# Self-attention probabilities transposed by VectorE blocks and SBUF transfers instead of TensorE, with a reordered step

## The chip, the cores and the metric

One core of a Trainium2 chip runs the whole kernel. The metric is device time in microseconds, median of several runs. Five engines run their own programs and meet only at semaphores: TensorE (PE, matrix products into PSUM), VectorE (DVE), ScalarE (ACT), GpSimd (POOL), and SP, which here issues nearly all DMA transfers, in the order of its program.

## The reference

64 sequences of 64 tokens with 512 features pass through one block of a transformer, everything in float32:

```python
x = x + xattn(layernorm(x), ctx, ctx, mask)   # 16 heads of 32, 512 context keys each
x = x + attn(layernorm(x))                    # self-attention over 64 tokens, 16 heads
x = x + ffn(layernorm(x))                     # relu(x W1 + b1) W2 + b2, W1 and W2 rounded to -1, 0, 1
```

The change lies in the second line. For each head q, k and v are projections with a bias, the scores are q k / sqrt(32), their softmax runs over 64 keys (the top-k mask keeps all 64), the probabilities multiply v, and the result goes through an output projection with a bias and is added to x.

## The kernel before

It has three stages, cross attention (to about 736 us), self attention (to about 1205 us) and FF, and every engine walks through them with a program of its own, written by hand, with explicit waits (`wait(e, semaphore, count)`). Nothing is scheduled by a planner: the order in `self_pe`, `self_act`, `self_dve`, `self_pool` and `self_sync` is the order in which the engines work.

The self stage goes through 16 units of four sequences, each in two tiles t = 0, 1 of 128 tokens (L447, `load_self_x`). Steps 0 and 1 stand out, a hardware loop runs steps 2 to 13, then come a last but one and a last step (`run_steps`). Step u is pipelined over three units: it attends in unit u, projects q, k and v of unit u+1, and makes the layer norm of unit u+2. Each projection is split into high and low parts, 12 or 24 products (`split_products`, L348), and goes to one of the banks `PJ`, whose turn is counted by `Banks`. Names of the products: Q0, Q1, K0, K1 (halves of the features), V0, V1, O0, O1 (tiles; O is the output projection). O1 of a unit is done in the next unit's step.

For one tile: `scores` on PE (L544), `self_maxima` on DVE (row maximum L519, subtraction L521), `self_exponentials` on ACT (L527), `self_divide` on DVE (sum L532, reciprocal, product L420), eight `transposes` of 128 x 128 on PE (L1460) into the PSUM pair PT, `probs_t_out` on ACT (L1596), which copies them to SBUF, `attend` on PE (L1481), `a_hi` and `a_lo`, which split the result into two parts (L1584 on ACT, L1657 and L1661 on DVE), and the O product. DVE adds O to the residual (`residual`, L1680), SP stores it (L1425).

The layer norm of unit u+2 takes, in step u: the load of x by SP (L447), statistics (L453) and aggregate on DVE, rstd on POOL (`rstd_of`, L1246), normalise (L465) and block transpose (L428) on DVE, a gather of four transfers on SP (L436), `x_hi` on ACT and `x_lo` on DVE (L556). POOL's step has two parts in this order, `self_residuals` for unit u+1, which adds x and the output bias into the buffer that unit u-1 has used and so waits for both stores of u-1, and then `rstd_of` for unit u+2:

```python
if kind != "last":
    self_residuals(e, later(u, 1))
if kind == "full":
    rstd_of(e, G.agg, G.eps, G.rstd, later(u, 2), NT, P)
```

In step u DVE works in the order: maxima (tile 0), residual O1 of u-1, statistics of u+2, divide (0), aggregate, maxima (1), normalise, a_hi and a_lo (0), divide (1), layer-norm transpose, K1 copy, V0 copy, two ternary columns of FF weights (L1301, L1304), V1 copy, x_lo, residual O0, a_lo (1). SP: load x of u+2, store (u-1, 1), layer-norm gather of u+2, store (u, 0). The cross stage already transposes its probabilities by DVE blocks of 32 x 32 (L1105) and four SBUF to SBUF transfers (L634).

## Time and profile before

| | us |
|---|---|
| median of 3 runs | 1671.46 (1671.02 to 1673.8) |
| profiled execution, its own time | 1671.81 |
| its span, first to last instruction | 1670.0 |
| mean granted TensorE clock | 0.988 of full |
| PE busy | 1604.1 (96%) |
| DVE busy | 1139.2 (68%) |
| ACT busy | 635.6 (38%) |
| POOL busy | 229.3 (14%) |

The span is that of one execution under the profiler. PE's busy share is an average over the three stages; what a change in one stage does is read in that stage, from which wait ends last there. A wait is put down to the engine or transfer whose signal came last.

### The profile page before, as it was taken

What the parts mean: (1) busy time and instruction counts of PE and PEld (TensorE: products, weight loads), DVE (VectorE), ACT (ScalarE), POOL (GpSimd) and SP (SyncE); (2) the same over time, 40 slices, a digit from 0 to 9 for tenths busy, and PEclk for the clock granted to TensorE, in tenths of its full rate; (3) what the DMA queues carried; (4) which work ended last, traced back from release to release, by engine and by line L of the source; (5) the groups of instructions that cost most, each with busy time, mean ns of one, the idle gap of its engine ahead of it and who ended that gap; (6) DMA issues with size and microseconds to landing.
All of it is one profiled execution on the core that took longest, in us unless ns stands there. A gap on an engine that the chain in (4) does not pass through costs nothing.

```text
span 1670.0 us, 37711 instructions
## 1 busy us (share of the span) xinstructions
PE 1604.1 (96%) x15500; PEld 1340.4 (80%) x15500; DVE 1139.2 (68%) x1556; ACT 635.6 (38%) x1593; POOL 229.3 (14%) x300
## 2 busy tenths in 40 slices
PE   5899999999999999969999999999799999999999
PEld 4678888888888887758888889888688888888887
DVE  3677777777777777856787777877686446555633
ACT  2555555555555555545222223222222222122221
POOL 1000000001111111311211112121122102202200
PEclk9999999999999999989999999999899999999999
DMA  6144444444444445463112121122212112211100
GB/s 228 39 113 116 115 113 113 113 115 118 116 116 113 113 114 139 145 236 96 46 51 63 38 69 44 50 63 77 58 51 69 58 26 76 63 57 31 51 26 26
DMA packets 120304, 144.61 MB, mean 87 GB/s; under 512 B 11936, under 2 KB 85792, under 8 KB 118944
## 3 DMA queue, kind: packets, MB, share of 16 engines
q1 hardware_dynamic: 120080, 139.32, 29.2%
q10 hardware_dynamic: 144, 4.19, 0.7%
q8 instruction: 53, 0.87, 0.2%
q14 instruction: 27, 0.22, 0.0%
HBM read 67.97 MB, written 25.17 MB: 56 GB/s over the span
## 4 chain that ended last, share of the span: by engine, by line
PE 87%; DVE 7%; DMA 2%; ACT 1%; issue 1%; SPq 1%; POOL 0%; DVEq 0%; ACTq 0%
PE project L348 49%; PE project L1351 14%; PE scores L1831 3%; PE scores L1829 3%; PE project L1831 3%; PE project L1829 3%; PE scores L775 3%; PE attended_t L794 2%; PE project L1460 2%; PE attended_t L1481 1%; DMA cross_probs_t<-cross_scores_probs 1%; PE scores L544 1%; SPq L634 1%; DVE cross_row_max L1088 1%; DVE self_at_lo L1661 1%
## 5 line engine op out<-in xcount | busy, mean ns | idle before, releaser
L1351 PE MATMUL project<-ff_xt,w_ternary 128*128 128x512 f32 x1024 | 253.1, 389 | 0.0
L1351 PEld LDWEIGHTS project<-ff_xt,w_ternary 128*128 128x128 f32 x1024 | 192.0, 188 | 39.8
L1361 ACT ACTIVATE hidden<-project,b_sb 128x512 f32<-128x512 f32 x128 | 88.2, 689 | 339.3 <-PE project L1351 339.3
L959 ACT ACTIVATE cross_scores_probs<-cross_scores_probs,exp_bias,logit_scale 128x128 f32<-128x128 f32 x256 | 123.0, 482 | 139.1 <-DVE exp_bias L1093 139.1
L348 PE MATMUL project<-self_xt_hi,self_w_hi 128*128 128x256 f32 x512 | 149.2, 291 | 2.4 <-DVE self_w_lo L408 2.4
L348 PE MATMUL project<-self_xt_lo,self_w_hi 128*128 128x256 f32 x512 | 146.2, 285 | 0.0
L348 PE MATMUL project<-self_xt_hi,self_w_lo 128*128 128x256 f32 x512 | 146.0, 285 | 0.0
L959 ACT ACTIVATE cross_probs<-cross_scores,exp_bias,logit_scale 128x128 f32<-128x128 f32 x256 | 122.8, 484 | 4.5 <-DVE exp_bias L1093 4.5
L348 PE MATMUL project<-ctx_hi,cross_w_hi 128*128 128x512 f32 x256 | 105.6, 412 | 15.8 <-DVE ctx_lo L1118 15.8
L348 PE MATMUL project<-cross_w_hi,ctx_hi 128*128 128x512 f32 x256 | 105.5, 412 | 0.0
L348 PEld LDWEIGHTS project<-self_xt_hi,self_w_hi 128*128 128x128 f32 x512 | 99.4, 194 | 4.9 <-issue 2.9
L348 PE MATMUL project<-ctx_hi,cross_w_lo 128*128 128x512 f32 x256 | 101.8, 398 | 0.0
L348 PE MATMUL project<-ctx_lo,cross_w_hi 128*128 128x512 f32 x256 | 101.5, 396 | 0.0
L1366 DVE CAST hidden_hi_a<-hidden 128x512 fp32r<-128x512 f32 x64 | 28.9, 452 | 105.4 <-ACT hidden L1361 105.3
L348 PE MATMUL project<-cross_w_lo,ctx_hi 128*128 128x512 f32 x256 | 100.5, 392 | 0.0
L481 POOL TENSOR_TENSOR self_residual<-self_x,bo_sb 128x512 f32<-128x512 f32 x32 | 53.9, 1708 | 335.6 <-DMA x<-self_residual 335.6
L348 PEld LDWEIGHTS project<-self_xt_lo,self_w_hi 128*128 128x128 f32 x512 | 99.4, 194 | 0.6
L348 PE MATMUL project<-cross_w_hi,ctx_lo 128*128 128x512 f32 x256 | 99.6, 389 | 0.0
L348 PEld LDWEIGHTS project<-self_xt_hi,self_w_lo 128*128 128x128 f32 x512 | 99.5, 194 | 0.0
L1366 DVE CAST hidden_hi_b<-hidden 128x512 fp32r<-128x512 f32 x64 | 28.7, 449 | 88.4 <-ACT hidden L1361 87.5
L1255 POOL TENSOR_TENSOR var_eps<-mean_var,ln_eps 128x2 f32<-128x2 f32 x16 | 5.1, 318 | 572.6 <-DVE mean_var L1055 572.6
L1596 ACT ACTIVATE self_probs_t<-project 128x1024 f32<-128x1024 f32 x32 | 32.9, 1027 | 123.8 <-PE project L1460 123.7
(172 smaller groups left out, 3994.9 us busy)
## 6 DMA issues: line engine op xcount, KB each, us to landing
ctx_raw<-in_ctx SPq DMA_DIRECT2D x64, 256.0 KB, 3.8
cross_probs_t<-cross_scores_probs SPq DMA_DIRECT2D x128, 128.0 KB, 2.6
cross_probs_t<-cross_scores SPq DMA_DIRECT2D x128, 128.0 KB, 2.7
cross_xt_raw<-in_x_t SPq DMA_DIRECT2D x64, 128.0 KB, 2.5
cross_x<-in_x SPq DMA_DIRECT2D x32, 256.0 KB, 3.2
x<-cross_x SPq DMA_DIRECT2D x32, 256.0 KB, 2.8
self_x<-x SPq DMA_DIRECT2D x32, 256.0 KB, 2.8
self_x_norm<-self_blocks_t SPq DMA_DIRECT2D x64, 128.0 KB, 2.7
```

The source lines that it names most:

```text
L348: last = nc.tensor.matmul(out_ap, a, b, start=(n == 0), stop=(n == 3 * len(pairs) - 1))
L481: e.tensor_tensor(sres[:, parity(v), t, :], sx[:, parity(v), t, :], bo_sb[:], ALU.add).then_inc(G.res, 1)
L775: last = nc.tensor.matmul(S[half:half + SEQ, slot * n:(slot + 1) * n], cq_t[rows, c, K.batch(q), :], keys, start=True, stop=True)
L794: last = nc.tensor.matmul(PV[rows, t, col:col + SEQ], cv[:, parity(u), q if K.kt == 1 else k, DK * head:DK * head + DK], probs_t[:, half:h ...
L959: last = nc.scalar.activation(c_p[buf][:, cols], c_s[buf][:, cols], ACT.Exp, bias=exp_bias[:, buf, g:g + 1], scale=logit_scale[:, parity(u ...
L1351: last = nc.tensor.matmul(PJ[m % 2][:], w1_q[:, c, cols], x_t[parity(v)][:, c].rearrange("p n a r -> p (n a r)"), start=(c == 0 and x_t is ...
L1361: nc.scalar.activation(h_raw[:, m % 2, :], PJ[m % 2][:], ACT.Relu, bias=b1_sb[:, m:m + 1]).then_inc(h_relu, 1)
L1366: nc.vector.tensor_copy(h_hi[m % 4], h_raw[:, m % 2, :]).then_inc(h_hi_ready, 1)
L1460: last = nc.tensor.transpose(PT[:, i * P:i * P + P], s_p[:, i * P:i * P + P], ident[:])
L1596: nc.scalar.activation(s_pt[:], PT[:], ACT.Copy).then_inc(G.pt_ready, 1)
L1829: nc.tensor.matmul(YB[t], h_hi[m % 4][:, rows], w2_q[:, m, :], start=(m == 0), stop=False)
L1831: last = nc.tensor.matmul(YB[t], h_lo[m % 4][:, rows], w2_q[:, m, :], start=False, stop=(m == FC - 1))
```

## The change

The transposes leave PE and ACT. The keys of a unit are stored interleaved (key 4k + j at place (j, k)); the exponentials are written in an order (j, head, k), the sum and the product follow it, DVE transposes blocks of 32 x 32 (`self_probs_blocks`) and SP moves the blocks to their places by four transfers (`self_probs_gather`); `attend` reads them there, from a buffer of its own for each tile. The PSUM pair that held the transposes becomes project banks 2 and 3 (`SB` with 4 banks). On PE, Q0 stands ahead of O1 of the unit before, K0 and K1 stand together, and so do V0 and V1; the waits of an attention stand ahead of the last product of K1 or O0. ACT takes the K1 copy and both `a_hi`. On DVE the residual of O1 comes after the block transposes of tile 0; layer-norm transpose ahead of divide (1). On SP the gathers come ahead of the stores. The last two steps are ordered anew: the last unit's first scores and V products move into the step before, and the first two hidden products of FF stand ahead of the last O0. `self_pool` isn't touched.

```diff
...
+            s_pt_0 = sb(st, "self_probs_t_0", [P, 1024])
+            s_blocks = sb(st, "self_probs_blocks", [P, 1024])
...
+            fxn_1 = sq_t[:, 0].rearrange("p c b s -> p (c b s)").rearrange("p (t d) -> p t d", t=2)
...
+        by_block = lambda a: a[:].rearrange("p (j g k) -> p j g k", j=4, k=16)
         def self_exponentials(e, u, t):
             wait(e, G.s_shifted, total(u, NT, t + 1))
+            wait(e, G.p_t, total(u, NT, t))
+            nc.scalar.activation(by_block(s_p).rearrange("p j g k -> p g j k"),
+                                 s_d[:].rearrange("p (g j k) -> p g j k", j=4, k=16),
+                                 ACT.Exp, scale=SCORE_SCALE).then_inc(G.p_ready, 1)
         def self_divide(e, u, t):
             wait(e, G.p_ready, total(u, NT, t + 1))
+            nc.vector.reduce_sum(row_sum[:], by_block(s_p).rearrange("p j g k -> p g j k"),
+                                 AXIS.XY).then_inc(G.p_sum, 1)
             wait(e, G.p_sum, total(u, NT, t + 1))
+            nc.vector.reciprocal(row_scale[:], row_sum[:]).then_inc(G.p_scale, 1)
+            wait(e, G.p_scale, total(u, NT, t + 1))
+            nc.vector.tensor_tensor(
+                by_block(s_p), by_block(s_p),
+                row_scale[:].unsqueeze(1).unsqueeze(3).to_broadcast([P, 4, HEADS, 16]),
+                ALU.mult).then_inc(G.p_norm, 1)
+        def self_probs_blocks(e, u, t):
+            wait(e, G.p_norm, total(u, NT, t + 1))
+            wait(e, G.pt_in[1 - t], total(u, 64, 64 * t))
+            blocks = lambda a: a[:].rearrange("p (m k) -> p m k", k=32)
+            nc.vector.transpose(blocks(s_blocks), blocks(s_p)).then_inc(G.p_t, 1)
+        def self_probs_gather(e, u, t):
+            wait(e, G.p_t, total(u, NT, t + 1))
+            wait(e, G.pv_done, total(u, NT))
+            for i in range(4):
+                e.dma_start(s_pt[t][:, 256 * i:256 * i + 256],
+                            s_blocks[32 * i:32 * i + 32, :]).then_inc(G.pt_in[t], 16)
...
+                to, of = dst[:, half, 2 * n + i, :, :], PJ[bank][:, 256 * i:256 * i + 256]
+                if name[0] == "K":
+                    to = to.rearrange("p b (j k) -> p b j k", k=16)
+                    of = of.rearrange("p (b k j) -> p b j k", b=4, k=16)
+                else:
+                    to = to.rearrange("p b s -> p (b s)")
+                last = nc.scalar.activation(to, of, ACT.Identity,
+                                            bias=bias[:, 2 * n + i:2 * n + i + 1])
...
+                self_probs_gather(e, S_FIRST, 0)
...
+                self_probs_blocks(e, S_FIRST, 0)
...
-        SB = Banks([], s_full_uses,
-                   ["Q0", "Q1", "K0", "K1", "O0", "O1"], ["V0", "V1", "O0"])
+        SB = Banks([], s_full_uses, ["Q0", "Q1", "K0", "K1", "O0", "O1"],
+                   ["V0", "V1", "H0", "H1", "O0"], 4)
...
                     load_self_x(e, later(u, 2))
+                if kind == "last":
+                    ff_ln_gather(e, F_FIRST, 1)
                 if not is_unit(u, 0):
+                    self_probs_gather(e, u, 0)
                     store(later(u, -1), 1, "last_but_one" if kind == "last" else "full")
                 if kind == "full":
...
-                    ff_ln_gather(e, F_FIRST, 1)
-                store(u, 0, kind)
+                self_probs_gather(e, u, 1)
                 if kind == "last_but_one":
                     ff_ln_gather(e, F_FIRST, 0)
+                store(u, 0, kind)
                 if kind == "last":
                     store(u, 1, kind)
...
-            def transposes(u, t):
-                wait(e, G.pt_ready, total(u, NT, t))
-                wait(e, G.p_norm, total(u, NT, t + 1))
-                for i in range(8):
-                    last = nc.tensor.transpose(PT[:, i * P:i * P + P], s_p[:, i * P:i * P + P],
-                                               ident[:])
-                last.then_inc(G.pt_full, 1)
...
-                wait(e, G.pt_ready, total(u, NT, t + 1))
+                wait(e, G.pt_in[t], total(u, 64, 64))
...
             def last_step(u):
                 before = later(u, -1)
+                scores(u, 1)
+                o_proj(before, 1, "last_but_one")
+                e.wait_ge(fxt_lo_ready, 2)
+                e.wait_ge(fw_ready, 2 * TERNARY_EARLY)
+                e.wait_ge(G.res, NT * S_UNITS)
+                bank, uses = SB.at(before, "O0", "last_but_one")
                 e.wait_ge(G.pj_free[bank], uses + 1)
+                ff_hidden(0)
                 attend_waits(u, 0)
                 attend(u, 0)
+                bank, uses = SB.at(before, "O1", "last_but_one")
+                e.wait_ge(G.pj_free[bank], uses + 1)
+                ff_hidden(1)
                 o_proj(u, 0, "last")
+                attend_waits(u, 1)
+                attend(u, 1)
+                e.wait_ge(G.at_lo, NT * S_UNITS)
+                o_products(LAST_O).then_inc(last_o_full, 1)
+                for name in ("V1", "O0"):
                     bank, uses = SB.at(u, name, "last")
                     e.wait_ge(G.pj_free[bank], uses + 1)
...
                 if not is_unit(u, 0):
+                    keys_ready(later(u, -1), "full")
                     scores(u, 0)
+                    qk_proj(u, "Q0", 0, kind)
                     o_proj(later(u, -1), 1, "full")
-                    qk_proj(u, "Q0", 0, kind)
                     qk_proj(u, "Q1", 0, kind)
                     scores(u, 1)
-                transposes(u, 0)
-                qk_proj(u, "K0", 1, kind, lambda: attend_waits(u, 0))
+                qk_proj(u, "K0", 1, kind)
+                qk_proj(u, "K1", 1, kind, lambda: attend_waits(u, 0))
                 attend(u, 0)
-                qk_proj(u, "K1", 1, kind)
                 if kind == "full":
                     v_proj(u, 0, kind)
-                    transposes(u, 1)
-                    v_proj(u, 1, kind, lambda: attend_waits(u, 1))
-                    attend(u, 1)
+                    v_proj(u, 1, kind)
                     if is_unit(u, 0):
                         e.wait_ge(sw_lo_ready[3], 1)
+                    o_proj(u, 0, kind, lambda: attend_waits(u, 1))
+                    attend(u, 1)
+                else:
+                    last = later(u, 1)
+                    keys_ready(u, kind)
+                    scores(last, 0)
+                    v_proj(last, 0, "last")
                     o_proj(u, 0, kind)
-                else:
-                    transposes(u, 1)
-                    o_proj(u, 0, kind)
+                    v_proj(last, 1, "last")
                     attend_waits(u, 1)
                     attend(u, 1)
...
                 qk_out(u, v, "Q1", kind)
                 magnitudes(u, 3, 6)
-                probs_t_out(u, 0)
                 self_exponentials(e, u, 1)
                 qk_out(u, v, "K0", kind)
+                qk_out(u, v, "K1", kind)
                 if is_unit(u, 0):
                     self_w_hi(e, 3)
-                magnitudes(u, 6, 9)
-                magnitudes(u, 9, 12)
-                probs_t_out(u, 1)
-                magnitudes(u, 12, 16)
+                a_hi(u, 0, kind)
+                magnitudes(u, 6, 12)
                 if kind == "full":
                     x_hi(u, later(u, 2))
-                a_hi(u, kind)
+                magnitudes(u, 12, 16)
+                if kind == "last_but_one":
+                    self_exponentials(e, v, 0)
+                a_hi(u, 1, kind)
...
             def last_step(u):
                 self_maxima(e, u, 1)
                 ff_ln_transpose(e, F_FIRST, 1)
+                self_divide(e, u, 0)
+                self_probs_blocks(e, u, 0)
                 ff_x_lo(e, F_FIRST, 0)
+                residual(later(u, -1), 1, "last_but_one")
+                ff_x_lo(e, F_FIRST, 1)
                 self_divide(e, u, 1)
+                self_probs_blocks(e, u, 1)
                 a_lo(u, 0)
+                ff_split_hidden(e, F_FIRST, 0)
                 residual(u, 0, "last")
+                ff_split_hidden(e, F_FIRST, 1)
                 a_lo(u, 1)
                 e.wait_ge(last_o_full, 1)
                 nc.vector.tensor_tensor(sres[:, parity(u), 1, :], LAST_O, sres[:, parity(u), 1, :],
                                         ALU.add).then_inc(last_o_free, 1)
...
+                if not is_unit(u, 0):
                     self_maxima(e, u, 0)
-                    residual(later(u, -1), 1, "full")
-                if kind == "full":
-                    self_ln_statistics(e, w)
-                    wait(e, G.stats, total(w, NT, NT))
+                self_ln_statistics(e, w)
+                wait(e, G.stats, total(w, NT, NT))
                 if not is_unit(u, 0):
                     self_divide(e, u, 0)
-                if kind == "full":
-                    self_ln_aggregate(e)
+                self_ln_aggregate(e)
                 if not is_unit(u, 0):
-                    self_maxima(e, u, 1)
-                if kind == "full":
-                    self_ln_normalise(e, w)
-                a_hi(u)
+                    self_probs_blocks(e, u, 0)
+                    residual(later(u, -1), 1, "full")
+                self_maxima(e, u, 1)
+                self_ln_normalise(e, w)
+                self_ln_transpose(e, w)
+                self_divide(e, u, 1)
+                self_probs_blocks(e, u, 1)
                 a_lo(u, 0)
-                self_divide(e, u, 1)
-                if kind == "full":
-                    self_ln_transpose(e, w)
-                keys_out(u, v, kind)
-                if kind == "full":
...
+                values_out(u, v, 0)
+                if not isinstance(u.half, int):
+                    for n in range(2):
+                        ternary(e, n, number(u) - 2, lambda k: total(u, 2, k - 4))
+                values_out(u, v, 1)
+                self_x_lo(e, w)
                 residual(u, 0, kind)
                 a_lo(u, 1)
...
```

## Rows read from the trace of the kernel before

**Rows 1.** Busy us of each engine by stretch: a steady step, the stage's last two, a pause.

```profile
core 0: us, PE busy (x) PEld busy (x) DVE busy (x) ACT busy (x) POOL busy (x), PEclk, DMA share, GB/s
967.71:996.96 29.25, 28.83 (x418) 25.57 (x417) 23.27 (x31) 8.37 (x12) 4.93 (x6) 1.00 0.18 54
1143.24:1205.27 62.03, 51.45 (x742) 43.65 (x741) 41.60 (x56) 16.03 (x21) 5.78 (x10) 0.92 0.26 78
...
1190.70:1197.00 6.30, 5.59 (x14) 4.35 (x15) 1.79 (x3) 0.00 (x0) 0.00 (x0) 0.50 0.00 0
```

**Rows 2.** Chain that ended last, in a steady step: start us, us, what.

```profile
979.12 1.02 PE project L1460 x8
...
994.04 3.00 PE project L348 x12
```

**Rows 3.** Timeline of DVE, a steady step: start, us, line, operation, out<-in, [idle before].

```profile
960.51 0.68 DVE L577 TENSOR_TENSOR self_v<-project,bv_sb 128x512 f32<-128x512 f32 x1
...
964.04 0.69 DVE L577 TENSOR_TENSOR self_v<-project,bv_sb 128x512 f32<-128x512 f32 x1
...
967.81 0.69 DVE L1680 TENSOR_TENSOR self_residual<-project,self_residual 128x512 f32<-128x512 f32 x1 [0.88 <-PE project L348]
...
970.30 1.22 DVE L521 TENSOR_TENSOR self_scores_shifted<-scores,row_max 128x1024 f32<-128x1024 f32 x1
...
973.05 1.28 DVE L453 BATCH_NORM_STATS2 ln_stats_buf<-self_x 128x6 f32<-128x512 f32 x2
...
975.91 1.82 DVE L420 TENSOR_TENSOR self_probs<-self_probs,row_scale 128x1024 f32<-128x1024 f32 x1
...
981.59 1.00 DVE L465 TENSOR_SCALAR self_x_norm<-self_x,mean_var,rstd 128x512 f32<-128x512 f32 x2
...
986.71 1.22 DVE L420 TENSOR_TENSOR self_probs<-self_probs,row_scale 128x1024 f32<-128x1024 f32 x1
```

**Rows 4.** Timeline of SP's DMA issues, same step.

```profile
968.69 0.36 SPq L1425 DMA_DIRECT2D x<-self_residual  x1
969.67 0.88 SPq L447 DMA_DIRECT2D self_x<-x  x2
973.19 0.35 SPq L1425 DMA_DIRECT2D x<-self_residual  x1
```

**Rows 5.** Timelines of SP and DVE in the cross stage, around two gathers.

```profile
522.67 2.49 SPq L634 DMA_DIRECT2D cross_probs_t<-cross_scores_probs  x4
525.42 0.40 SPq L640 DMA_DIRECT2D x<-cross_x  x1
...
525.71 1.25 DVE L1105 STREAM_TRANSPOSE cross_scores<-cross_probs 128x1024 f32<-128x1024 f32 x1
...
531.74 1.23 DVE L1083 TENSOR_TENSOR cross_scores<-scores,mask_bias 128x1024 f32<-128x1024 f32 x1 [0.36 <-DMA cross_probs_t<-cross_scores]
```

**Rows 6.** Timeline of POOL, the same steady step and the last step but one.

```profile
975.35 3.52 POOL L481 TENSOR_TENSOR self_residual<-self_x,bo_sb 128x512 f32<-128x512 f32 x2 [24.20 <-DMA x<-self_residual]
...
979.88 0.55 POOL L1246 TENSOR_TENSOR rstd<-var_eps,minus_half 128x1 f32<-128x1 f32 x1
...
1150.73 2.90 POOL L481 TENSOR_TENSOR self_residual<-self_x,bo_sb 128x512 f32<-128x512 f32 x2 [24.04 <-DMA x<-self_residual]
```

**Rows 7.** DMA issues: tensors, queue, count, KB each, median us from issue to landing.

```profile
x<-cross_x SPq DMA_DIRECT2D x32, 256.0 KB, 2.8
self_x<-x SPq DMA_DIRECT2D x32, 256.0 KB, 2.8
```

**Rows 8.** Timeline of PE: products that follow an idle time, in brackets.

```profile
750.42 1.94 PE L1460 MATMUL project<-ident,self_probs 128*128 128x128 f32 x8 [3.65 <-DVE self_probs L420]
...
791.15 1.13 PE L544 MATMUL scores<-self_k_t,self_q_t 32*64 32x64 f32 x32 [0.43 <-DVE thresholds L1762]
...
969.28 0.47 PE L348 MATMUL project<-self_w_hi,self_at_hi 128*128 128x512 f32 x1 [0.42 <-DVE self_at_lo L1661]
...
1191.41 0.76 PE L348 MATMUL project<-self_w_hi,self_at_hi 128*128 128x512 f32 x1 [4.22 <-DVE self_at_lo L1661]
```

## What I predict, and why

> **What bounds the kernel now.** I read first the busy table of one steady step of the self stage, then the chain that ended last through it, then each engine's timeline in it with the waits named there. TensorE (PE) is busy 28.83 of a step's 29.25 us at full clock, VectorE (DVE) 23.27, ScalarE 8.37, GpSimd (POOL) 4.93 [rows 1]. So PE bounds the step today. The chain says the same: project products and two groups of eight transposes, about 1.0 us each (one stands) [rows 2], with a gap of 0.4 us ahead of O1 [rows 8]. The trap is in who comes second. A step of unit u also prepares the layer norm of u+2, and this runs through four engines: DVE adds O1 of u-1 to the residual, SP stores it, POOL waits for the store, overwrites that buffer for u+1, and only then computes the rstd of u+2, which DVE needs to normalise. POOL's wait for that store fills 24.2 us of a step [rows 6]. Today the chain just fits: the store is issued at 973.19, POOL starts at 975.35, its last rstd ends at 979.88 + 0.55 = 980.43, and DVE normalises at 981.59, with 1.2 us to spare [rows 3, 4, 6].
>
> **The change part by part.** All times are of the profiled execution (1671.81 us, span 1670.0; 0.35 us above the median of the three runs, 1671.46). B is the end of the block transposes of a unit's second tile, T the start of the next unit's first scores.
>
> PE. The transposes leave: 2 x 1.0 us a step [rows 2], and Q0 ahead of O1 covers the 0.4 us gap [rows 8]. Floor of the step for PE: 29.25 - 2.0 - 0.4 = 26.8 us.
>
> ScalarE and DVE. ScalarE loses two evictions of the transposes and takes the K1 copy and the first high half of the attention; at 8.37 of 29.25 us it hides them. DVE gains two block transposes of about 1.24 us (the same instruction with the same shape, [rows 5]) and gives away about 1.5 us of copies: about 24.2 us of work a step. The four project banks take away no wait, since no product of the step waits for an eviction; I price them at nothing, and the cover is PE's own products. The reordered exponential, sum and product have the same number of elements, but no row shows their layout. Nearest rows: the plain product at 1.22, one stretched by POOL at 1.82 [rows 3]. I take 1.22 (same element count, no second engine) and keep 1.2 us a step for two of them as the upper end; a gain is excluded because the element count stands.
>
> Latency of one tile's turn. Blocks end at 525.71 + 1.25 = 526.96; the reader that waits for the gather starts at 531.74: 4.8 us, of which 2.49 is SP issuing four transfers [rows 5]. On a queue with nothing else this sits behind PE's products. The Trainium skill (VectorE: DVE Perf Modes, Rules for kernel authors) advises TensorE for a 128x128 transpose whose result may go to PSUM, which speaks against this change. By that rule one would keep the 2.0 us on PE for a shorter turn; by the rows here the turn becomes 1.24 + 4.8 = 6.0 us, which costs only where it lies on a loop.
>
> What is moved. Here lies the price. Residual O1 goes behind the divide and the block transposes of tile 0 on DVE; its store goes behind the gather of tile 0 on SP; POOL's program is not touched, so its wait for that store still stands ahead of the rstd, and behind the rstd stand, on DVE in this order, normalise, layer-norm transpose, divide and blocks of tile 1. That is a loop from one B to the next:
>
> 1. After B, DVE does a_lo of tile 0 (0.6, a copy like V1's), V0 and two ternary columns (964.04 - 960.51 = 3.5, with a little waiting for PE in it, so 3.4), V1 (0.6) and x_lo (1.2, as many elements as the product), then residual O0: it starts at B + 5.8 [rows 3].
> 2. Its store is issued 0.88 later, the loads of x for u+2 0.83 behind that (0.98 in this row, less in others), the second 0.44 later, and it lands 2.8 after its issue [rows 4, 7]: 5.0. DVE itself is ready for the statistics earlier (residual, a_lo, maxima: 970.30 + 1.22 - 967.81 = 3.7 after the residual's start [rows 3]), so the load is late by 1.3. Statistics at B + 10.8; bound below B + 9.5.
> 3. Statistics, sum and reciprocal 975.91 - 973.05 = 2.86, product 1.22, blocks 1.25, and 0.2 for the aggregate between: 5.5 [rows 3, 5].
> 4. Four gather issues and the gap to the store: 525.42 - 522.67 = 2.75 [rows 5]. The store then needs 2.16 until POOL starts when alone (975.35 - 973.19); the like store of the cross stage, which also stands behind a gather, lands only after 2.8 [rows 4, 6, 7]. So 4.9 to 5.6; I take 5.3, between, because that stage moves more data beside it.
> 5. POOL: two residuals 2.90 when DVE is not in its way, against 3.52 when it is, plus 980.43 - 978.87 = 1.6 for the two rstd: 4.5 [rows 6]. DVE stands idle there, so I take 2.90.
> 6. Second normalise 0.5 (half of a pair's 1.00), layer-norm transpose 1.2, sum and reciprocal 1.6 (2.86 less 1.28), product 1.22, blocks 1.25: 5.8 [rows 3, 5].
>
> Sum: 10.8 + 5.5 + 5.3 + 4.5 + 5.8 = 31.9 us from B to B. It does not pass through PE at all, and it is longer than PE's 26.8 and than today's 29.25. Bounds: 30.2 if the load of x is not late and the store is quick (9.5 + 5.5 + 4.9 + 4.5 + 5.8); 33.1 with the slow store (+0.3), POOL's 3.52 (+0.6) and 0.3 from the clock (next).
>
> On point 5 the Trainium skill (SBUF — State Buffer, Who interferes with whom) says that VectorE and GpSimd share one port pair which the first to start holds for its whole instruction. The trace agrees in direction only: the product grew by 0.6 us, not by a whole POOL instruction. By the rule alone, with DVE in the way once a step, the loop would be half of 2.90, 1.45 us longer, and the time some 17 us higher.
>
> PE's clock. PE now idles about 4 us a step, from the end of V1 to O0, which waits for a_lo behind the blocks. After an idle of 4.22 us at the stage's end the granted clock was 0.50 (the lower level, 1.2 GHz) through the 12 products of O that followed, which take 3.00 us at full clock [rows 1, 2, 8]; at half clock I count 5.4 to 6. O0 starting at B + 0.7 would end at about B + 6.1, 0.3 after the point in 1: nearly all of it is hidden behind the gather.
>
> Steps 2 to 13 lie between 791.15 and 1143.24 today, 352.1 us for 12 [rows 1, 8]. After: step 2 finds its x in time and takes about 1.0 less, the others 31.9 each: 12 x 31.9 - 1.0 = 381.8, so +29.7 (9 to 44 over the bounds).
>
> Opening. The wait of 3.65 us ahead of the first unit's second transposes goes [rows 8], since no product stands behind them until the attention; step 1 pays the loop for the first time, 31.9 - 29.25 = 2.7. Sum -1, bounds -4 and +2.
>
> Stage end. From the first scores of the last unit but one to the last O products, 62.03 us pass today, PE busy 51.45 of them at a mean clock of 0.92 [rows 1]. The longest wait in it is that of 4.22 us [rows 8]. The new order takes out four groups of transposes, 4 us, and this wait, but FF's first hidden products wait for both halves of x, whose second gather (4.8) and low half now stand behind the divide and blocks of the last unit on DVE; I count 34 us to the last O1, 8 us of new idle, then hidden, O0, hidden, attention and last O in 16 to 18: about 59. So -3, bounds -6 and +2.
>
> Sum: +29.7 - 1 - 3 = +26 on 1671.8, 1697.5 as a median.
>
> **The rivals.** (A) PE stays the bound at 26.8 a step, because POOL's rstd is not late: 352.1 - 12 x 26.8 = 30 off, 5 off the opening, 3 off the end: 1634 us. For it: PE is 99% busy today, DVE would need only 24.2 of 26.8, and today's trace shows no normalise that waits for POOL. It decides from the point where the loop is under 26.8, that is 5.1 us shorter than my sum and 3.4 shorter than its lower bound; against it, every leg is a row of this trace. Chance 0.10. (B) The loop bounds, but at its lower end, the load of x and the store not late: 30.2 a step, 1671.8 + 9 - 1 - 3 = 1677; with a better end it falls within no change. Chance 0.15 (a third of it no change). (C) The loop is longer, 33 us and more: DVE products stretched by the new layout (1.2 a step), or the half clock reaching the attention as well; 1671.8 + 43 - 4 = 1711, up to 1720. Chance 0.15. My forecast itself, 31 to 32.6 a step, 1687 to 1706: 0.60.
>
> **How the numbers follow.** The likeliest is 1697.5. For 8 in 10 I leave out A and the top of C and take in the bounds: 1674 to 1716. A measurement of this kernel tells about 0.2% (3.3 us) from no change. Faster by more than that: A, 0.10. Within: 0.05 from B. Slower: 0.85.
>
> **What would show it.** In the steady step of after: the normalise of the layer norm waits about 5 us for POOL rstd; POOL's residual starts some 16 us after T instead of 7.6; no transposes on PE, and PE idles 4 to 5 us a step, ahead of O0 or the attention, with a granted clock under 1 there; statistics wait about 1 us for the DMA of x. The step's length is read from first scores to first scores: 31.9. I am wrong if POOL's residual starts within 10 us of T, if normalise doesn't wait, or if PE shows no idle time in the step; then A holds.

## The result and the profile after

The changed kernel takes 1712.75 us (median of 4 runs, 1711.41 to 1713.81) against 1672.41 us before: a ratio of 1.024, 95% interval 1.022 to 1.026. It is slower, by 40 us, and inside the range forecast (1674 to 1716), 15 us above the likeliest value. The profiled execution has a span of 1710.6 us against 1670.0. Split where the prediction split it, by the first scores of a unit on PE:

| part | before | after | difference | forecast |
|---|---|---|---|---|
| to the first scores of step 2 | 791.15 | 797.95 | +6.8 | -1 |
| steps 2 to 13 | 352.09 | 386.69 | +34.6 | +29.7 |
| stage end, to the last O | 62.03 | 61.20 | -0.8 | -3 |

So the steady steps carry the loss. The page of after, its busy times and its chain that ended last:

```profile
PE 1595.5 (93%) x15244; PEld 1326.3 (78%) x15244; DVE 1144.0 (67%) x1542; ACT 621.5 (36%) x1607; POOL 219.5 (13%) x300
...
PE 66%; DVE 15%; DMA 7%; issue 4%; SPq 4%; POOL 2%; ACT 2%; DVEq 0%; POOLq 0%; ACTq 0%
```

A third of the chain lies off PE. Here are the busy times by stretch, after: one steady step, the eleven steps 3 to 13, and three times the O0 of a step alone (columns as in [rows 1]).

```profile
992.41:1024.29 31.88, 28.61 (x400) 24.96 (x400) 23.37 (x30) 7.33 (x13) 4.13 (x6) 0.95 0.31 82
830.00:1184.64 354.64, 315.27 (x4407) 274.51 (x4401) 258.49 (x331) 82.53 (x143) 45.47 (x66) 0.94 0.32 82
...
858.01:863.10 5.09, 5.09 (x12) 3.77 (x13) 4.57 (x7) 1.06 (x1) 0.00 (x0) 0.54 0.46 103
1018.96:1023.50 4.54, 4.50 (x12) 3.23 (x12) 4.20 (x7) 1.06 (x1) 0.00 (x0) 0.62 0.50 116
890.64:896.03 5.39, 5.39 (x12) 3.77 (x12) 4.56 (x7) 1.06 (x1) 0.00 (x0) 0.50 0.43 97
```

Before, the same eleven steps took 29.26 us each:

```profile
821.43:1143.24 321.81, 317.24 (x4578) 281.27 (x4577) 255.58 (x341) 91.96 (x132) 54.10 (x66) 1.00 0.19 54
```

The step is 31.88 us, the forecast 31.9; the mean of the eleven is 32.24. The transposes are gone from PE, but it is not the bound any more: it waits 2.7 to 4.7 us ahead of O0 in each of the eleven steps (nine of them are in the last line of the next table). In the three steps shown O0's 12 products then run at a granted clock between 0.50 and 0.62 (1.2 GHz for most of them) and take 4.5 to 5.4 us instead of 3.00 [rows 2]. Who waits for whom between 850 and 1140 us (us in total, times, longest):

```profile
POOL self_residual L484 <- DMA x<-self_residual: 250.1, 9, 28.3
...
DVE self_x_norm L468 <- POOL rstd L1282: 59.1, 19, 7.0
...
PE project L351 <- DVE self_at_lo L1687: 29.5, 9, 4.7
```

And the loop itself, in the timelines of DVE, SP and POOL (start, us), from the block transposes of one unit's second tile to the next. It answers to [rows 3, 4, 6].

```profile
1017.03 1.25 DVE L556 STREAM_TRANSPOSE self_probs_blocks<-self_probs 128x1024 f32<-128x1024 f32 x1
...
1023.83 0.68 DVE L1701 TENSOR_TENSOR self_residual<-project,self_residual 128x512 f32<-128x512 f32 x1
...
1028.78 1.29 DVE L456 BATCH_NORM_STATS2 ln_stats_buf<-self_x 128x6 f32<-128x512 f32 x2 [0.61 <-DMA self_x<-x]
...
1032.95 1.21 DVE L556 STREAM_TRANSPOSE self_probs_blocks<-self_probs 128x1024 f32<-128x1024 f32 x1
1034.08 0.65 DVE L1701 TENSOR_TENSOR self_residual<-project,self_residual 128x512 f32<-128x512 f32 x1
...
1043.09 0.55 DVE L468 TENSOR_SCALAR self_x_norm<-self_x,mean_var,rstd 128x512 f32<-128x512 f32 x1 [5.31 <-POOL rstd L1282]
...
1048.68 1.25 DVE L556 STREAM_TRANSPOSE self_probs_blocks<-self_probs 128x1024 f32<-128x1024 f32 x1
```

```profile
1034.19 2.50 SPq L564 DMA_DIRECT2D self_probs_t<-self_probs_blocks  x4
1036.89 0.44 SPq L1464 DMA_DIRECT2D x<-self_residual  x1
```

```profile
1039.76 2.52 POOL L484 TENSOR_TENSOR self_residual<-self_x,bo_sb 128x512 f32<-128x512 f32 x2 [27.45 <-DMA x<-self_residual]
...
1043.30 0.75 POOL L1282 TENSOR_TENSOR rstd<-var_eps,minus_half 128x1 f32<-128x1 f32 x1
```

This is one closed chain. The block transposes of tile 0 end at 1034.16, and the four gather issues behind them hold SP until 1036.69. So the store of O1, whose residual is ready at 1034.73, is issued only at 1036.89; POOL starts at 1039.76 when it has landed; the rstd ends at 1044.05, then comes normalise, and at 1048.68 the blocks of tile 1, with which the next round begins. Before, POOL was done 1.2 us ahead of need; now DVE waits 5.3 us for it.

### The profile page after: what moved, and what is told of

The parts are those of the page before. It is cut to its first block, busy times and chain, and to the rows that moved or that the text cites. A ratio compares the mean times of both kernels' runs of the same rounds, so it can differ in the third digit from the quotient of the medians.

```text
span 1710.6 us, 37206 instructions
## 1 busy us (share of the span) xinstructions
PE 1595.5 (93%) x15244; PEld 1326.3 (78%) x15244; DVE 1144.0 (67%) x1542; ACT 621.5 (36%) x1607; POOL 219.5 (13%) x300
## 4 chain that ended last, share of the span: by engine, by line
PE 66%; DVE 15%; DMA 7%; issue 4%; SPq 4%; POOL 2%; ACT 2%; DVEq 0%; POOLq 0%; ACTq 0%
PE project L351 32%; PE project L1387 14%; PE scores L1858 3%; PE scores L1856 3%; PE project L1858 3%; PE project L1856 3%; PE scores L810 3%; SPq L564 2%; DMA x<-self_residual 2%; DVE row_sum L540 2%; PE attended_t L829 2%; DVE self_probs L545 2%; DVE self_probs_blocks L556 1%; DMA cross_probs_t<-cross_scores_probs 1%; DVE self_blocks_t L431 1%
## 5 line engine op out<-in xcount | busy, mean ns | idle before, releaser
L351 PE MATMUL project<-self_w_hi,self_at_hi 128*128 128x512 f32 x124 | 58.5, 472 | 49.1 <-DVE self_at_lo L1687 45.1
L484 POOL TENSOR_TENSOR self_residual<-self_x,bo_sb 128x512 f32<-128x512 f32 x32 | 40.8, 1297 | 392.7 <-DMA x<-self_residual 392.7
```

The lines of the kernel that those rows point to most:

```text
L351: last = nc.tensor.matmul(out_ap, a, b, start=(n == 0), stop=(n == 3 * len(pairs) - 1))
L484: e.tensor_tensor(sres[:, parity(v), t, :], sx[:, parity(v), t, :], bo_sb[:], ALU.add).then_inc(G.res, 1)
```

## The experiments

Each ran as the changed kernel with the edit shown, unless it says otherwise. Ratios are to the kernel before, with their 95% interval. A step is the mean of steps 3 to 13.

**1. GpSimd computes the rstd ahead of the residuals.** If the loop is what I say, this cuts its legs of store and residual out.

```diff
-                if kind != "last":
-                    self_residuals(e, later(u, 1))
                 if kind == "full":
                     rstd_of(e, G.agg, G.eps, G.rstd, later(u, 2), NT, P)
+                if kind != "last":
+                    self_residuals(e, later(u, 1))
```

> The changed kernel with one edit: GpSimd computes the two rstd of unit u+2 ahead of the two residuals of u+1, which wait for the store. My theory (the loop through residual O1, its store, GpSimd's wait and the rstd sets the step): the legs of store (2.7 + 2.9 us) and residuals (2.5) leave the way to the normalise, so that B to B is 10.5 + 5.4 + 1.6 for the rstd, part of it hidden, + 5.9, some 23 us, under PE's 26.8. PE then bounds: 26.9 us a step instead of 32.2, twelve steps, -64, and about -1 in the opening: 1648 us (1640 to 1662); the normalise no longer waits for rstd. Rival (the longer turn of a tile, block transposes and gather, 6 us against 2 of transposes and eviction, sets the step by PE's own waits for the probabilities): the swap takes only about 2 us off a step, 1690 us (1680 to 1705), and PE goes on waiting 4 us a step ahead of O0 and the attention. Second rival (VectorE and GpSimd hinder each other, now that they run side by side): 28 to 29 us a step, 1662 to 1675.

Measured: 1644.4 us, ratio 0.984 (0.983 to 0.986). The busy times of one step and of the eleven:

```profile
1011.76:1038.55 26.79, 26.79 (x400) 23.98 (x400) 23.90 (x30) 7.35 (x13) 3.99 (x6) 1.00 0.38 98
...
822.61:1119.53 296.92, 295.46 (x4407) 264.53 (x4401) 262.63 (x331) 82.72 (x143) 44.82 (x66) 1.00 0.38 97
```

A step is 296.92 / 11 = 26.99 us, PE is busy in all of it at full clock, and the wait of normalise for the rstd is gone from the list. Two lines swapped on an engine that is 13% busy turn a loss of 40 us into a gain of 27. Both rivals fall: a tile's longer turn doesn't bound, and neither do VectorE and GpSimd side by side.

**2. The same swap in the kernel before**, as a control.

> The kernel before with the same swap on GpSimd, rstd ahead of the residuals. There my account has the rstd 1.2 us early and PE busy 99%: no change, 1672 (1669 to 1675). Were the wait for the store already part of what sets the time before the change, this would be faster by more than 5 us.

Measured: 1673.14 us, ratio 1.0015 (1.0005 to 1.0026): not faster, and at most a quarter of a per cent slower. The order on GpSimd cost nothing until the change moved the residual of O1 and its store back.

**3. More work on GpSimd inside the loop**, a third addition between the residuals and the rstd. It writes a spare buffer and changes no output.

```diff
-            sb(st, "self_gap_3", [P, 512])
+            spare = sb(st, "self_gap_3", [P, 512])
...
+                    wait(e, G.pt_ready, total(u, 1))
+                    e.tensor_tensor(spare[:, 0:D], sx[:, parity(later(u, 1)), 1, :], bo_sb[:],
+                                    ALU.add).then_inc(G.pt_ready, 1)
                     rstd_of(e, G.agg, G.eps, G.rstd, later(u, 2), NT, P)
```

> The changed kernel with one more addition of 128x512 on GpSimd between the residuals and the rstd (into a spare buffer), in 14 steps. By my theory every microsecond there lengthens the loop: half of the pair's 2.52 us is 1.26, in the twelve steps 2 to 13 that is +15 us, up to +18 with steps 0 and 1: 1728 us (1725 to 1732). By the rival of the longer turn, GpSimd is no part of what bounds, and has slack: no change, 1713 (1710 to 1716). If VectorE also ran slower beside it, more than 1735.

Measured: 1731.78 us, ratio 1.037 (1.035 to 1.039): +19. The addition takes 1.30 us, a step became 370.70 / 11 = 33.70, that is 1.46 longer. The rest, 0.16, goes with PE's clock: behind 4.2 us of idle O0 ran at a granted clock of 0.52, and the residual of O0 on DVE, which starts the loop, waited for it, in 8 of the eleven steps (4.6 us together) where in after it waits in 3 (1.5):

```profile
1051.62 1.30 POOL L1801 TENSOR_TENSOR self_gap<-self_x,bo_sb 128x512 f32<-128x512 f32 x1
```

```profile
1066.67 0.69 DVE L1701 TENSOR_TENSOR self_residual<-project,self_residual 128x512 f32<-128x512 f32 x1 [0.48 <-PE project L351]
```

**4. The store of O1 ahead of the gather on SP.**

```diff
                 if not is_unit(u, 0):
+                    if kind == "full":
+                        store(later(u, -1), 1, "full")
                     self_probs_gather(e, u, 0)
-                    store(later(u, -1), 1, "last_but_one" if kind == "last" else "full")
+                    if kind != "full":
+                        store(later(u, -1), 1, "last_but_one" if kind == "last" else "full")
```

> The changed kernel with the store of O1 of u-1 ahead of the gather of tile 0 on SP, instead of behind it; VectorE's order is untouched, so the gather waits 1.2 us longer for the residual. By my theory the store is issued at about 1.4 instead of 2.73 us after the blocks of tile 0, and lands in 2.2 to 2.9: -1.3 to -2.0 us a step, twelve steps: -20, 1693 us (1688 to 1698). By the rival of the longer turn the gather's own delay of 1.9 us is paid each step and nothing is gained: +10 to +20, 1725 to 1735.

Measured: 1673.71 us, ratio 1.002 (1.001 to 1.003): -39 against the changed kernel, twice what I expected. The step is 321.52 / 11 = 29.23, 3.0 less. The store and GpSimd's start:

```profile
1038.31 0.36 SPq L1467 DMA_DIRECT2D x<-self_residual  x1
1038.84 2.50 SPq L564 DMA_DIRECT2D self_probs_t<-self_probs_blocks  x4
```

```profile
1040.48 2.55 POOL L484 TENSOR_TENSOR self_residual<-self_x,bo_sb 128x512 f32<-128x512 f32 x2 [24.95 <-DMA x<-self_residual]
```

The blocks end at 1037.56, so the store is issued 0.75 behind them instead of 2.73, and lands in 2.17 instead of 2.87: -2.7, where I had allowed the residual 1.2 us that it doesn't take (0.65). The rest I did not isolate; in these steps PE's mean granted clock rose from 0.94 to 0.99 and the residual of O0 waits for PE in none of them, and the opening gave 4.8 us too. Direction and place are as the theory has them; the size was missed. The rival would have made this slower.

**5. The load of x ahead of the store of O0 on SP** (that store moves behind the loads of the next step).

```diff
                 if kind == "full" and not is_unit(u, 0):
                     load_self_x(e, later(u, 2))
+                if not is_unit(u, 0) and kind != "last":
+                    store(later(u, -1), 0, "full")
...
-                store(u, 0, kind)
+                if kind != "full":
+                    store(u, 0, kind)
```

> The changed kernel with SP's loads of x for u+2 ahead of the store of O0 of u-1, instead of behind it; nothing else moves. The statistics of the layer norm, a leg of the loop by my theory, wait 0.6 to 0.8 us a step for this load; then they start when VectorE is ready: -0.6 to -0.8 in each of eleven or twelve steps, -8, 1705 us (1702 to 1708), and the wait of the statistics for the DMA of x is gone from the trace. Rival (the loop closes elsewhere, the load is no part of it): no change, 1713.

Measured: 1699.53 us, ratio 1.017 (1.016 to 1.019): -13, more than the 5 to 11 expected. The step is 343.92 / 11 = 31.27, and the statistics wait for nothing:

```profile
1049.35 1.28 DVE L456 BATCH_NORM_STATS2 ln_stats_buf<-self_x 128x6 f32<-128x512 f32 x2
```

They start 9.98 us after the blocks before them (1039.37) instead of 10.50 and 10.77 in two neighbouring steps. This leg, too, is on the loop. That it gave more than 8 us goes with 3.4 us in the opening and, it seems, with the clock again (0.97 against 0.94; the residual of O0 waits for PE in none of the eleven steps); this wasn't isolated.

**6. The load of w2 behind the first unit's gathers.** It asks why the opening lost 6.8 us where I had it gain one. In the trace of after, SP and PE in the opening:

```profile
744.28 0.34 SPq L1468 DMA_DIRECT2D ff_w_raw<-in_w  x1
744.91 2.79 SPq L439 DMA_DIRECT2D self_x_norm<-self_blocks_t  x4
748.83 8.38 SPq L564 DMA_DIRECT2D self_probs_t<-self_probs_blocks  x4
```

```profile
751.98 0.79 PE L351 MATMUL project<-self_w_hi,self_at_hi 128*128 128x512 f32 x1 [3.93 <-POOL self_w_lo L411]
760.16 0.70 PE L351 MATMUL project<-self_w_hi,self_at_lo 128*128 128x512 f32 x1 [3.13 <-DMA self_probs_t<-self_probs_blocks]
```

```diff
                 self_probs_gather(e, u, 1)
+                if is_unit(u, 0):
+                    e.dma_start(w_raw[:, 1].rearrange("p k n -> p (k n)"), w2) \
+                        .then_inc(fw_in[1], 16)
...
-            e.dma_start(w_raw[:, 1].rearrange("p k n -> p (k n)"), w2).then_inc(fw_in[1], 16)
             run_steps(e, S_UNITS, step)
```

> The changed kernel with the load of w2 (4 MB) behind the two gathers of the first unit on SP's queue, instead of ahead of them. The opening took 8 us more than I had summed: the gather of the probabilities was issued in 8.4 us instead of 2.5, PE waited 3.1 us for it and ScalarE 6.9 us for the gather of the layer norm. By my theory they stood behind the 4 MB: the first scores of step 1 come 3 to 4.5 us earlier, the step behind it a little more, 1708 us (1705 to 1710). Rival (the wait of O0 for the low half of the O weights on GpSimd, 3.9 us, and what follows from it sets the opening): the attention then waits less but nothing else moves, 1711 to 1713.

Measured: 1711.56 us, ratio 1.024 (1.023 to 1.026): no change, a miss, and inside the rival's range. The trace shows why; the theory's first half holds, and the rival's "nothing else moves" does not. On SP, PE and DVE:

```profile
747.80 2.50 SPq L564 DMA_DIRECT2D self_probs_t<-self_probs_blocks  x4
750.34 0.59 SPq L1452 DMA_DIRECT2D ff_w_raw<-in_w  x1
...
755.19 0.90 SPq L450 DMA_DIRECT2D self_x<-x  x2
```

```profile
754.70 1.16 PE L573 MATMUL scores<-self_k_t,self_q_t 32*64 32x64 f32 x64
...
771.87 0.39 PE L351 MATMUL project<-self_xt_hi,self_w_hi 128*128 128x256 f32 x1 [3.19 <-DVE self_residual L1703]
```

```profile
765.87 1.29 DVE L456 BATCH_NORM_STATS2 ln_stats_buf<-self_x 128x6 f32<-128x512 f32 x2 [7.29 <-DMA self_x<-x]
```

The gather is issued in 2.50 us and step 1 begins at 754.70 instead of 761.90: 7.2 us earlier, about where my sum had it (759.51 - 3.65 = 755.9). Of these, 3.1 are the wait for the gather itself; 1.0 is an earlier start of O0; and 3.0 are PE's clock: in after, O0 and the attention take 9.92 us from 751.98, 6.8 of them without that wait, at a mean granted clock of 0.67, here 3.74 us at 1.00. Then the next thing on the queue, the load of x, stands behind the same 4 MB (13.6 us from issue to landing in this trace); statistics wait 7.29 us and PE 3.19, and step 2 begins at 796.65 against 797.95. In both places the 4 MB hold up what stands behind them. No run took them out of the opening altogether.

**7. Both edits together**, to see whether the second adds to the first.

> Both edits: rstd ahead of the residuals on GpSimd, and the load of w2 behind the first unit's gathers. With the rstd first the opening's O0 waits 6.7 us for a product on VectorE that took 5.1 instead of 1.2 us beside GpSimd's low half of the O weights, and the gather only 0.7 more: so the load of w2 costs less here, 1 to 2 us, 1643 us (1640 to 1645). If the 4 MB held the opening by themselves, -5: 1639.

Measured: 1650.12 us, ratio 0.987 (0.986 to 0.989): a miss by 7 us, and no faster than the first edit alone. The same wait for x came (7.89 us in the same place), and step 2 began at 795.61 against 792.43. The move of w2 is no gain in either kernel.

**8. FF's statistics behind the last unit but one's block transposes**, on top of both. It asks why the stage end gave 0.8 us instead of 3. In the trace of after, DVE waits for FF's x ahead of the second tile's probabilities, and PE behind that:

```profile
1203.34 2.47 DVE L1348 BATCH_NORM_STATS2 ln_stats_buf<-ff_x 128x6 f32<-128x512 f32 x4 [5.23 <-DMA ff_x<-x]
```

```profile
1210.87 0.76 PE L351 MATMUL project<-self_w_hi,self_at_hi 128*128 128x512 f32 x1 [4.32 <-DVE self_at_lo L1687]
...
1231.28 3.69 PE L1387 MATMUL project<-ff_xt,w_ternary 128*128 128x512 f32 x8 [7.75 <-DVE ff_xt L1380]
```

```diff
                 self_maxima(e, u, 1)
-                ff_ln_statistics(e, F_FIRST)
-                e.wait_ge(f_stats, FT)
-                ff_ln_aggregate(e)
                 self_divide(e, u, 1)
                 self_probs_blocks(e, u, 1)
                 a_lo(u, 0)
+                ff_ln_statistics(e, F_FIRST)
+                e.wait_ge(f_stats, FT)
+                ff_ln_aggregate(e)
```

> As the kernel with both edits, and in the last unit but one VectorE computes the FF statistics behind the divide, the block transposes and the low half, instead of ahead of them. In the kernel with the rstd first these statistics wait 5.3 us for the load of x for FF, and behind them stand the probabilities for which PE idles 4.4 us at the stage's end. My sum had given the stage end -3, the trace of the changed kernel gives -0.8; by my reading this stall is the difference: PE's wait of 4.4 us goes, the FF layer norm comes 2 us earlier, stage end -2 to -4, 1640 us (1638 to 1642). Rival (the two gathers and low halves of FF's x behind it set the end whatever comes ahead): within 1 us of the kernel with both edits, 1643.

Measured: 1647.55 us, ratio 0.986 (0.985 to 0.988), 2.6 under experiment 7 and less than the spread of the runs; the trace shows the gain: from the first scores of the last unit but one to the end of the span 522.3 us instead of 525.95. The median lies 7.5 us above the one expected, as experiment 7, from which it starts, did by 7. Without the move of w2:

> The rstd ahead of the residuals on GpSimd, the load of w2 where the changed kernel has it, and FF's statistics behind the block transposes of the last unit but one. The move of w2 gave nothing behind the first two steps, the move of the statistics took 3.6 us off the stage end (from the first scores of the last unit but one to the end of the span: 525.95 to 522.3). So 3 us under the kernel with the rstd first alone (1644.4): 1641 us (1639 to 1644), under both kernels.

Measured: 1639.58 us (5 runs), ratio 0.981 (0.980 to 0.982): faster than both kernels. PE in its stage end:

```profile
1147.14 0.47 PE L351 MATMUL project<-self_w_hi,self_at_hi 128*128 128x512 f32 x1 [0.99 <-DVE self_at_lo L1687]
1158.73 3.78 PE L1387 MATMUL project<-ff_xt,w_ternary 128*128 128x512 f32 x8 [8.60 <-DVE ff_xt L1380]
```

The wait of 4.4 us is down to 1.0, and the stage end to the end of the span is 521.7 us instead of 526.9 in experiment 1; the wait for the low half of FF's x, the longest in both, went from 7.7 to 8.6. What would shorten it wasn't tried.

**9. O1 ahead of Q0 again**, in the kernel of experiment 1, where PE bounds. It prices that part of the change.

```diff
                     scores(u, 0)
-                    qk_proj(u, "Q0", 0, kind)
                     o_proj(later(u, -1), 1, "full")
+                    qk_proj(u, "Q0", 0, kind)
```

> The kernel with the rstd first, but with O1 of the other unit ahead of Q0 again, as in the kernel before. There PE bounds at 26.99 us a step. By my sum Q0's new place covers the wait of 0.4 us ahead of O1: without it PE waits 0.2 to 0.4 us a step for the low half, steps 27.2 to 27.4, +2.5 to +5: 1648 us (1646 to 1650). Rival (VectorE's low half comes before O1 in either order, since PE now starts the scores later than VectorE needs): no change, 1644.

Measured: 1648.7 us, ratio 0.986 (0.984 to 0.987). The two times alone hardly tell 4 us; the traces do. The step is 301.17 / 11 = 27.38 instead of 26.99: Q0's place is worth 0.39 us, near the gap of 0.42 ahead of O1 in [rows 8]. Of the 4.25 us in eleven steps, 2.9 are listed as PE's waits for that low half.

## Why the prediction was right, and where its sizes were off

- **The loop.** Right, and shown by taking a leg out (1), lengthening one (3) and shortening two (4, 5): the time follows each. Leg by leg, forecast and measured in the step shown: residual of O0 at B + 5.8, 5.55; statistics at B + 10.8, 10.50 (10.77 in the step before); to the end of the blocks of tile 0 +5.5, 5.38; to GpSimd's start +5.3, 2.73 + 2.87 = 5.60; GpSimd 4.5, 4.29; to the next B +5.8, 5.88. Sum 31.9, against 31.65 from B to B here, and 31.88 and 31.96 from first scores to first scores in two steps.
- **The signs** came as named, two of them smaller: normalise waits 5.3 us (about 5 forecast), POOL's residuals start 15.5 us after the first scores (16), the statistics wait 0.6 us (about 1), and PE idles 3.3 us in the step shown, 3.6 in the mean (4 to 5).
- **The mean of the steps** is 0.34 above the sum, 3.7 us over the eleven. In one step, of 34.28 us, the store took 4.5 us to POOL's start instead of 2.9, and in three the residual of O0 waits for O0 at half clock, 1.5 us together. So the half clock is hidden behind the gather in most steps, as I had said, but not in all. Why that one store was slow, no run shows. With step 2, which I made 1.0 shorter than a step and which took 32.05, steps 2 to 13 exceed the forecast by five us.
- **PE's floor.** 26.8 forecast, 26.99 measured in experiment 1; 2.0 for the transposes and 0.4 for Q0 were about the right prices: experiment 9 gives 0.39 for Q0's place, which leaves 1.9 for the rest (29.26 to 27.38). The Trainium skill (VectorE: DVE Perf Modes, Rules for kernel authors) advises TensorE for such transposes; here, where PE bounds, moving them to DVE and SP takes 1.9 us off a step, once no loop runs through their turn. Rival A described that kernel: its 1634 is 6 us under the 1639.58 of experiment 8.
- **The opening** is the step that failed: -1 with an upper bound of +2, measured +6.8. I took the wait of 3.65 us away and asked who else waits there, but not what stands ahead of the new gather on SP's queue: 4 MB of w2, issued 0.6 us before the layer norm's gather (8.8 us in the kernel before). Experiment 6 shows this for the 7.2 us up to step 1, half clock included, and that they come back in step 1 if w2 is only put behind the gather. PE's wait for the low half of the O weights (3.93) is a second cover that was too short: product O0 comes earlier now (751.98 against 756.56), and GpSimd ends that low half later (751.93 against 749.18), as ScalarE's high half starts 2.6 us later, behind the exponentials and now also the K1 copy. And step 1 pays the loop more dearly than the 2.7 us allowed: it takes 36.05 us against 31.64 before. With the rstd first (experiment 1) it takes 29.59, and step 2 begins at 792.43, so that the swap gives back 5.5 of the 6.8 us, although the 4 MB stand where they stood. How the loss divides between the 4 MB and the loop stays open.
- **The stage end**: -3 forecast within -6 and +2, -0.8 measured. The idle time of 8 us was right (7.75); the 4.32 us behind the load of FF's x were not in the count, and experiment 8 took 3.6 us back.
- **The layout** of the exponential, sum and product cost nothing, as taken: 1.06, 1.22 and 1.22 us in the step shown. The four banks nothing either: among PE's waits in steps 3 to 13 none is for an eviction.
- **GpSimd and VectorE on one port.** I wrote that the trace agrees with the Trainium skill (SBUF — State Buffer, Who interferes with whom) in direction only, since the product grew by 0.6 us. That was misread, as the last section shows. The loop didn't pay it only because DVE stands idle while GpSimd runs.

The time fell into rival C's band (1711 to 1720), though the loop of a steady step was the forecast's, 31.9 and not 33: it is the terms beside the loop that were off. The 15 us are about 8 from the opening, 5 from the steps and 2 from the end.

## What to carry to other kernels

When work is moved behind other work, list on every queue what stands behind it and follow that list until it closes: here a store behind a gather made a wait on an engine that is 13% busy the bound of a kernel whose first engine was 99% busy in that step. Then look in that loop for work which doesn't need the wait that it stands behind; two lines in another order gave 68 us. A new small transfer is priced with what is already in its queue, a large load above all.

## What the runs showed of the hardware

**A VectorE instruction with two inputs in SBUF waits out the running GpSimd one.** The product takes 1.23 us alone. In the opening of experiment 1 it met GpSimd's low half of the O weights, and in a steady step the second of the residuals:

```profile
748.26 4.53 POOL L411 TENSOR_TENSOR self_w_lo<-self_w_raw,self_w_hi 128x2048 fp32r<-128x2048 f32 x1 [2.49 <-ACT self_w_hi L405]
...
1026.98 2.54 POOL L484 TENSOR_TENSOR self_residual<-self_x,bo_sb 128x512 f32<-128x512 f32 x2 [5.17 <-DMA x<-self_residual]
```

```profile
748.75 5.12 DVE L545 TENSOR_TENSOR self_probs<-self_probs,row_scale 128x1024 f32<-128x1024 f32 x1
...
1026.28 1.25 DVE L431 STREAM_TRANSPOSE self_blocks_t<-self_x_norm 128x1024 f32<-128x1024 f32 x1
1027.45 1.18 DVE L540 TENSOR_REDUCE row_sum<-self_probs 128x16 f32<-128x1024 f32 x1
...
1028.95 1.65 DVE L545 TENSOR_TENSOR self_probs<-self_probs,row_scale 128x1024 f32<-128x1024 f32 x1
```

GpSimd ends at 752.79 and 1029.52; from there the product needs 1.08 us both times, and 1.07 to 1.09 in the nine other steady steps of this trace in which the product starts while GpSimd runs. The 1.82 us of [rows 3] read the same way: the first residual of that pair ends at 975.35 + 1.26 = 976.6, 0.7 after the product's start, and 1.1 remain; and the pair took 3.52 us instead of 2.54 because its second waited for the product in turn. The Trainium skill (SBUF — State Buffer, Who interferes with whom) states this: an instruction of VectorE with two inputs in SBUF blocks against one of GpSimd that reads SBUF, one with a single input and outside the two-port modes doesn't. The traces agree: what the product takes longer is the rest of the running GpSimd instruction, and the transpose and the sum, with one input, took their usual 1.25 and 1.18 us beside the residuals.

**A transfer behind others on its queue lands later.** The store took 2.17 us to GpSimd's start ahead of the four gather transfers (experiment 4), 2.87 behind them (after). Over all stores of a trace, those of O0 included, median from issue to landing (KB each, us), in experiment 4:

```profile
x<-self_residual SPq DMA_DIRECT2D x32, 256.0 KB, 2.0
```

In after it is 2.8. Behind the load of 4 MB, four gather issues took 8.38 us in after; ahead of it, in experiment 6, 2.50.
